# A Mamba-style block between two half feed-forward layers, one core: second operands of GpSimd's operations shifted by one word, and a fourth of six gated products moved off VectorE

## What is computed

```python
x = x + 0.5 * ffn(layernorm(x))          # FFN 1
x = x + ssm(layernorm(x))                # convolution, gate, selective scan
x = x + 0.5 * ffn(layernorm(x))          # FFN 2, the same weights

def ffn(x):                              # 256 -> 768 -> 256
    h = silu(x @ wg.T) * (x @ wu.T)
    return h @ wd.T

def ssm(x):
    z, params = x @ W_z.T, x @ W_params.T
    dt = softplus(params[..., :64] @ W_dt.T + b_dt)
    u = silu(causal_conv4(x))
    # for each of 256 channels and 16 states, over the 1024 steps:
    #   h = exp(dt*A) * h + (exp(dt*A)-1)/A * u ;  y += C * h
    return ((y + u * D) * silu(z)) @ W_out.T
```

## Time and profile before

| what | us |
|---|---|
| median of 3 executions | 2335.79 (2335.43 to 2336.45) |
| the profiled execution | 2332.63 |
| its span, first to last instruction | 2330.8 |
| PE busy in it | 2127.4 (91%) |
| DVE busy | 2170.3 (93%) |
| ACT busy | 1978.8 (85%) |
| POOL busy | 2088.6 (90%) |
| mean granted clock of TensorE, of full speed | 0.979 |

### The profile page before, as it was taken

One profiled execution on the slowest core, in us unless ns is written; L12 is line 12 of the kernel. 1 busy time (PEld: TensorE's weight loads), 2 busy tenths in 40 slices (PEclk: granted clock), 3 DMA queues, 4 the chain that ended last, 5 costly groups with the idle time before them and its releaser, 6 DMA issues. The chain is left out here.

```text
span 2330.8 us, 27774 instructions
## 1 busy us (share of the span) xinstructions
PE 2127.4 (91%) x8708; PEld 1279.3 (55%) x8708; DVE 2170.3 (93%) x2361; ACT 1978.8 (85%) x2876; POOL 2088.6 (90%) x1382
## 2 busy tenths in 40 slices
PE   7886999999999999999999999999999999998578
PEld 3452556555565655656555565655556465555246
DVE  2499999999999999999999999999999999999993
ACT  5988898898989889898988989898898989888772
POOL 2588999999999999999999999999999999999773
PEclk9997999999999999999999999999999999999779
DMA  2122434444343443444444444434434344433221
GB/s 89 38 77 69 136 136 137 145 135 147 129 143 136 137 144 128 144 144 137 140 136 143 134 129 155 145 135 138 141 131 137 141 150 136 137 127 118 74 63 37
DMA packets 112024, 291.15 MB, mean 125 GB/s; under 512 B 11201, under 2 KB 45314, under 8 KB 111874
## 3 DMA queue, kind: packets, MB, share of 16 engines
q1 hardware_dynamic: 111874, 289.35, 37.1%
HBM read 271.49 MB, written 17.83 MB: 124 GB/s over the span
## 5 line engine op out<-in xcount | busy, mean ns | idle before, releaser
L1105 POOL TENSOR_TENSOR acc<-acc,ring 128x1024 f32<-128x1024 f32 x512 | 1209.5, 2362 | 57.5 <-DVE ring L1301 40.9
L1265 DVE TENSOR_TENSOR_SCAN g_bank<-du_bank,ring 128x1024 f32<-128x1024 f32 (+1 forms) x512 | 1098.1, 2150 | 8.8 <-ACT du_bank L1008 6.3
L778 PE MATMUL work<-wd_t,hid 128*128 128x256 f32 x3072 | 680.6, 380 | 7.2 <-DVE hid L1218 6.1
L1301 DVE SCALAR_TENSOR_TENSOR ring<-g_bank,inv_a,ring 128x1024 f32<-128x1024 f32 (+1 forms) x576 | 662.2, 1155 | 12.4 <-POOL acc L1105 3.6
L778 PEld LDWEIGHTS work<-wd_t,hid 128*128 128x128 f32 x3072 | 583.4, 190 | 107.7 <-issue 15.2
L1026 ACT ACTIVATE ring<-dt,a_coef 128x1024 f32<-128x1024 f32 (+1 forms) x576 | 575.2, 1046 | 9.6 <-DVE g_bank L1265 8.4
L845 ACT ACT_TABLE_LOAD x271 | 347.7, 1283 | 4.9
L909 ACT ACTIVATE sil<-work 128x512 f32<-128x512 f32 x384 | 222.8, 599 | 111.6 <-PE work L766 110.7
L766 PE MATMUL work<-xt_hi,wg_t 128*128 128x512 f16 x768 | 296.0, 385 | 22.4 <-ACT sil L909 8.0
L766 PE MATMUL work<-xt_hi,wu_t 128*128 128x512 f16 x768 | 296.1, 386 | 21.7 <-ACT sil L909 14.4
L766 PE MATMUL work<-xt_lo,wg_t 128*128 128x512 f16 x768 | 295.4, 385 | 0.0
(11 more groups left out here) (98 smaller groups left out, 2693.4 us busy)
## 6 DMA issues: line engine op xcount, KB each, us to landing
ring<-c_rows SPq DMA_DIRECT2D x448, 512.0 KB, 3.7
ring<-c_rows SPq DMA_DIRECT2D x64, 256.0 KB, 3.2
x_in<-L_attn_x SPq DMA_DIRECT2D x30, 512.0 KB, 3.9
out<-x_fin SPq DMA_DIRECT2D x30, 512.0 KB, 5.0
x_fin<-L_attn_x SPq DMA_DIRECT2D x2, 512.0 KB, 5.9
c_rows<-params SPq DMA_DIRECT2D x32, 32.0 KB, 3.6
out<-x_in SPq DMA_DIRECT2D x2, 512.0 KB, 2.9
ring<-L_ffn_w_gate SPq DMA_DIRECT2D x1, 768.0 KB, 5.8
```

What stands on the lines that cost most here:

```text
L778: last = pe.matmul(dst[:, j * E:(j + 1) * E], hid[:, K.unit[f, bt, c, m] % HIDS, t:t + P], wd_t[:, m, :], start=(m == 0), stop=(m == HM - 1))
L1105: nc.gpsimd.tensor_tensor(v, v, shaped(bt, cg[:, K.number[ev[1:]] % TERMS, :]), ALU.add).then_inc(S["summed"], 1)
L1265: scan = nc.vector.tensor_tensor_scan(g, du_h, d_h, first[0], ALU.add, ALU.mult)
L1301: nc.vector.scalar_tensor_tensor(v, g, inv_a[:, h, s:s + 1], c_row, ALU.mult, ALU.mult).then_inc(S["weighted"], 1)
```

## The change

It has two parts.

**One word past.** `x_mid`, `sil`, `zs`, `sp_v` and the part `cg` of the ring now start one float32 word (4 bytes) past a multiple of eight words. They are the second operand of POOL's large operations (`cm`, `gate`, `hp`, `dp`, `ra`; in `rp` the two operands change places so that `x_mid` is the second). Small constants are packed into one tensor to make room. No instruction is added or taken away by this part.

**A fourth product.** m = 1 goes from `OWN` to `POOLED`. For each of the 64 chunks (16 batches, two FFNs, two chunks) one `sh` on DVE becomes one `sc` on ACT plus one `hp` on POOL. The `sc` takes the place in the list that the `sh` had; the `hp` gets a place of its own a little later.

```diff
-POOLED = (0, 2, 4)
-OWN = (1, 3, 5)
+POOLED = (0, 1, 2, 4)
+OWN = (3, 5)
+SKEW = 8
...
-    "sc1": [-35.454, -30.319, -27.9, -25.339, -22.957, -22.372],
-    "hp1": [-33.45, -29.15, -28.37, -23.334, -22.643, -22.332],
-    "sh1": [-32.255, -29.294, -26.295, -24.381, -20.683, -19.854],
+    "sc1": [-35.454, -32.255, -30.319, -27.9, -25.339, -24.381, -22.957, -22.372],
+    "hp1": [-33.45, -31.455, -29.15, -28.37, -23.334, -23.324, -22.643, -22.332],
+    "sh1": [-29.294, -26.295, -20.683, -19.854],
...
+        def skewed(name, *shapes):
+
+            sizes = [int(np.prod(shape[1:])) for shape in shapes]
+            t, first, views = sb(name, [P, 1 + sum(sizes)]), 1, []
+            for shape, size in zip(shapes, sizes):
+                views.append(t[:, first:first + size].rearrange("p (a n) -> p a n", a=shape[1]))
+                first += size
+            return views
...
-        x_mid = [sb(f"x_mid{i}", [P, NC * TJ, E]) for i in range(2)]
+        x_mid = skewed("x_mid", [P, NC * TJ, E], [P, NC * TJ, E])
...
-        sil = sb("sil", [P, SILUS, CH])
+        sil, zs, sp_v = skewed("odd", [P, SILUS, CH], [P, EH, L], [P, 2, CH])
...
+        decay, cg = slots(0, DECAYS), slots(DECAYS * L + 1, TERMS)
+        spread = slots((DECAYS + TERMS) * L + SKEW, SPREADS)
...
-                    nc.gpsimd.tensor_tensor(v, v, x_of(bt)[:, t, :].rearrange("p j e -> p (j e)"),
+                    nc.gpsimd.tensor_tensor(v, x_of(bt)[:, t, :].rearrange("p j e -> p (j e)"), v,
                                             ALU.add).then_inc(S["mid_added"], 1)
```

More of the change, by code:

```diff
@@ L233 @@
         -19.556],
-    "sc1": [-34.092, -30.866, -30.177, -27.991, -24.029, -21.873],
-    "hp1": [-32.649, -31.494, -27.862, -27.819, -23.185, -22.75],
-    "sh1": [-31.186, -30.505, -27.478, -27.372, -22.129, -20.873],
+    "sc1": [-34.092, -31.186, -30.866, -30.177, -27.991, -27.372, -24.029, -21.873],
+    "hp1": [-32.649, -30.386, -31.494, -27.862, -27.819, -26.572, -23.185, -22.75],
+    "sh1": [-30.505, -27.478, -22.129, -20.873],
     "dn1": [-23.737, -23.191, -17.748, -16.383],
@@ L524, in macaron_kernel @@
         du = sb("du", [P, L])
-        sil = sb("sil", [P, SILUS, CH])
+        sil, zs, sp_v = skewed("odd", [P, SILUS, CH], [P, EH, L], [P, 2, CH])
         hid = sb("hid", [P, HIDS, CH])
-        zs = sb("zs", [P, EH, L])
         u = [sb(f"u{i}", [P, EH, 2 + L]) for i in range(2)]
@@ L531, in macaron_kernel, with slots @@
         params = sb("params", [P, L])
-        ring = sb("ring", [P, DECAYS + TERMS + SPREADS, L])
-        decay, cg, spread = ring[:, 0:DECAYS, :], ring[:, DECAYS:DECAYS + TERMS, :], ring[:, DECAYS + TERMS:, :]
+        ring = sb("ring", [P, (DECAYS + TERMS + SPREADS) * L + SKEW])
+        def slots(first, count):
+            return ring[:, first:first + count * L].rearrange("p (s n) -> p s n", s=count)
+        decay, cg = slots(0, DECAYS), slots(DECAYS * L + 1, TERMS)
+        spread = slots((DECAYS + TERMS) * L + SKEW, SPREADS)
         acc = [sb(f"acc{i}", [P, EH, L]) for i in range(2)]
@@ L536, in macaron_kernel @@
         sp_r = sb("sp_r", [P, 2, CH])
-        sp_v = sb("sp_v", [P, 2, CH])
         wg_t = sb("wg_t", [P, EH, HID], F16)
@@ L549, in macaron_kernel @@
         part_ident = sb("part_ident", [P, P], F16)
-        ones = sb("ones", [P, 1])
-        minus_half, eps = sb("minus_half", [P, TJ]), sb("eps", [P, TJ])
+        consts = sb("consts", [P, 2 * TJ + 1 + EH + 1])
+        minus_half, eps = consts[:, 0:TJ], consts[:, TJ:2 * TJ]
+        ones, d_skip = consts[:, 2 * TJ:2 * TJ + 1], consts[:, 2 * TJ + 1:2 * TJ + 1 + EH]
         a_coef = sb("a_coef", [P, EH, N])
@@ L555, in macaron_kernel @@
         kept = sb("kept", [P, EH, N])
-        d_skip = sb("d_skip", [P, EH])
         carry = sb("carry", [P, 2, N, EH, 1])
-        flag = sb("flag", [1, 1], I32)
+        flag = consts[0:1, 2 * TJ + 1 + EH:].bitcast(I32)
         flag_f = stats[0:1, 0, 0, 0:1]
         inv_a_u = hid[:, 0, 0:EH * PROWS].rearrange("p (h n) -> p h n", h=EH)
-        flat = ring[:].rearrange("p s n -> p (s n)").bitcast(I32)
+        flat = ring[:, 0:DECAYS * L].bitcast(I32)
         st_g = flat[:, 0:EH * HID].rearrange("p (k m) -> p k m", k=EH)
```

## The result

The changed kernel takes 2381.82 us (median of four executions, 2374.21 to 2387.45), the kernel before beside it on the same chip 2336.12 (2335.43 to 2336.47). The ratio is 1.0201, interval 1.0187 to 1.0216: slower by 46 us, 9 us above the forecast of 2373 and inside its range. The profiled execution took 2376.70 us, its span is 2374.9, and its mean granted clock 0.976 (before: 0.979).

What follows compares the result with a forecast made beforehand. The bound was a closed path over PE, ACT and DVE, mostly PE. Lag of 2.75 us per batch over 14 batches gave 38.5, less 1, so profiled 2332.6 became 2370; median 3.2 above, 2373, range 2330 to 2388.

Steps and rivals of the forecast that it cites:

- The bound: A closed path sets the batch time: PE about 107 of 137 us with excursions to ACT, DVE 30.
- rival 1: DVE is the bound and the bank no matter; each `sh` gone gains 0.59 us, giving 2301; chance 0.17.
- The stall: FFN 1, chunk 0, m = 1: ACT's `sc` behind `db` frees the bank late; `dn` starts 2.85 us later.
- What takes it up: PE's gap at 1198.18 absorbs 0.17 idle and 0.17 drained matmul end, leaving 2.51; DVE then waits 1.6 us.
- rival 2: The stall comes but is taken up on the way as ACT and PE shift: 2331 to 2343; chance 0.12.
- The `sc` ahead of ACT's run: Chunk 1's `sc` precedes ACT's unbroken run from 1223.20, for which PE waits at 1229.42: +0.50 us per batch.
- The `sh` off DVE's path: FFN 2, chunk 0, between 1241.63 and 1271.50: its `sh` leaves DVE's part of the path, -0.59 us per batch.
- The last `sc`: FFN 2, chunk 1: its `sc`, ahead of the one at 1302.74, lengthens PE's wait for ACT, +0.33 us per batch.
- The sum: Net lag over one batch, carried round into the next: 2.75 us.
- The start: 14 periods of 2.75 us, batches 2 to 15; 1 us off because batch 2 meets a shorter stall.
- The shift: POOL's large operations lose 467 ns at 1024 columns, 182 at 512; worth 0 us steady, bound 4 overall.
- Rival 3: The shift does nothing; POOL has 135.4 us of work under a 139.8 us path: 2373 to 2388; chance 0.05.

Runs made afterwards that it cites:

- one_moved: Changed kernel with only the product of FFN 1, chunk 0, m = 1 moved, operands shifted: 2381.73 us, ratio 1.0212.
- late_sh: Kernel before, but DVE issues the `sh` of FFN 1, chunk 0, m = 1 just ahead of the half's first scan: 2372.57 us, ratio 1.0167.
- three_moved: Changed kernel, but the product of FFN 1, chunk 0, m = 1 stays on DVE, other three moved: 2342.12 us, ratio 1.0036.
- path_only: Changed kernel with only the product of FFN 2, chunk 0, m = 1 moved, operands shifted: 2329.12 us, ratio 0.9978.
- path_two: Changed kernel, only FFN 2, chunk 0, m = 1 moved, its `sc` earlier, plus m = 3 there in batches 2 to 13: 2322.74 us, ratio 0.9952.
- product_only: Kernel before with the fourth product moved and the old layout, no operand shifted: 2466.44 us, ratio 1.0569.

## Why the prediction was right, and where it was not

**The bound.** Right. A closed path over several engines sets the period: 24 us less DVE work and 206 less POOL work go with 46 us more time. DVE as the bound (rival 1, 2301) falls with one_moved and late_sh. One size was wrong without a consequence: each `sh` gone takes 0.37 us off DVE's busy time (24 us for 64) and not 0.59, so that DVE stands at 132.9 us per period and not at 131.8.

**The stall.** Predicted 2.85, measured 2.84, for the reason given; late_sh makes it with no work moved and three_moved removes it with one product left in place.

**What takes it up.** I had 0.34 taken up at PE's next gap and a wait of 1.6 us at DVE's next `sh`; the trace has 1.56. The gap took exactly the 0.34: the matmul at 1198.18 before starts at 1224.92 after, a lag of 2.49. Up to the next `up` only 0.05 more is taken up, and rival 2 (2331 to 2343) falls.

**The `sc` ahead of ACT's run.** Predicted +0.50; PE's wait there went from 0.71 to 1.18, +0.47.

**The `sh` off DVE's path.** This step failed in its size. The sum had -0.59; path_only measures -0.20. Between DVE's wait at 1241.63 and its release of PE at 1271.50 I saw no wait, and took the stretch for DVE's own. But in it lies a scan that reads ACT's `db`, with 0.25 us to spare. The lag in the table above says the same: 2.91 ahead of that scan, 2.69 at it. Behind the scan a `sh` does count in full: path_two.

**The last `sc`.** Predicted +0.33; PE's wait for ACT went from 1.50 to 1.71, +0.21.

**The sum.** 2.84 - 0.34 + 0.47 - 0.20 + 0.21 = 2.98, less the 0.05 taken up later is 2.93, and the period grew by 2.93 where I had 2.75. That the miss is so small is in part luck: the `sh` on DVE's path was 0.39 too good, and the `sc` terms were together 0.15 too dear.

**The start.** I had 14 such periods less 1, or 37.5 us. There are 13 of 2.90, or 37.7, and 7 us at the start, which no step of mine had; that 37.5 and 37.7 agree so well is luck. The shorter stall of batch 2 that I took 1 off for is there (PE waits 2.41 us at 240.48), but the kernel before has a wait of 2.83 us for ACT close behind it, at 239.12, which the changed kernel has not, and PE's lag goes only from 5.9 us ahead of the stall to 6.8 behind both. Most of the 7 us is there sooner: DVE's scans lag by 5.1 us (172.26 to 177.32) from the middle of batch 0 on, where a scan waits 1.89 us for `db` and not 0.19. Up to 1.7 us of these come from a `dn` for whose end ACT waits ahead of that `db`: it takes 7.13 us and not 5.45, at a granted clock of 0.66 from 155 to 160 us, where the kernels of before, one_moved and three_moved have 1.00. Three products give 303.1 us at the second `db` of batch 1, one product 300.7 and the shift alone 300.8, against 298.9 before and 305.9 after: the one `sc` by itself does not make the loss of the start, and what makes the rest of it stays open.

**The shift.** Worth 0 in the steady part: right. It leaves the period at 137.07 and takes 3.5 us off elsewhere, within the bound of 4. Its size on POOL was not right. I took 1895 ns for all large operations from `du<-u`, whose inputs are neighbours in one tensor; `cm` measures 1998, so 364 ns each instead of 467, and POOL stands at 117.6 us per period and not at 114. The odd write of DVE costs nothing (1277 ns against 1275 over 448 operations).

**Rival 3** (the shift does nothing: 2373 to 2388). I excluded it rightly, but priced it wrongly: without the shift the product takes 2466. I compared sums of busy time, 135.4 us of POOL under a period of 139.8, and so counted POOL's room as if it could be used anywhere. In fact an `hp` holds a slot of `sil` that a silu of ACT waits for. Putting the slots of `sil` at 0 was right only in the shifted layout.

## What to carry over

In a kernel whose order is fixed, ask of every moved instruction what it frees, and where the new engine stands in its own queue when that is wanted: here 2.84 us of lateness of one bank, once a batch, cost most of the loss. Leaving that one product alone took back 40 of the 46 us, and one number in a table 21. A gain on an engine's stretch of the path ends at the first operand that another engine delivers just in time, so look in the stretch for producers that end a few tenths before they are read, not only for waits. And compare loads of an engine only together with what it releases: POOL was idle for 12% of the unshifted kernel with the product moved, and that kernel was still 85 us slower than the shifted one.

## What the hardware showed

**GpSimd and the distance of its operands.** A two-input float32 operation of 128x1024 takes 2339 ns in line and 1996 with the second operand 1 or 2 words (modulo 4) past the first; at 512 columns 1262 and 1088. Neighbouring words of one tensor give 1889 and 1036. The Trainium skill, GPSIMD Engine Reference, section 3.1, calls 4497 ns for 2048 elements the floor of two inputs, from which an estimate for 1024 is 2250. No run here has 2048 elements, but a straight line through the in-line times, 1262 for 512 and 2339 for 1024, gives an estimate of 4493 for them. So the page's figure agrees with the placement in line, and the runs with another placement go below it: as a floor of two inputs it does not hold here.

**The granted clock in mid-kernel.** In slices of 10 us from 300 to 2150 us the kernel before and the one with the shift alone show a granted clock of 1.00 in every one. In one_moved, with PE waiting 2.84 us each batch, it falls below that in some batches only (a mean of 0.72 of the full 2.4 GHz over 6 us, so part of them at the lower level of 1.2 GHz), after that wait, and periods with it are 1.4 to 3.1 us longer than the shortest; in product_only its mean over the run is 0.943. The wait alone does not decide it. The changed kernel's trace has the same wait of 2.84 us in 13 batches and shows 1.00 in every such slice, while three_moved has no wait at that `dn` and falls to 0.83 in single slices, one of them behind a wait of PE of 1.71 us for ACT (at 488.89). What tells these batches apart is not shown. It may be that the spread of the changed kernel (2374 to 2387 us; mean clock 0.978 in the shortest execution, 0.972 in the two longest) is such a fall in some executions, but the two longest have no trace, and that is not shown.
